# LoRA B rows packed into three operands filled by indirect DMAs, and the h sums moved to GpSimd

## The reference

```python
def lora_linear(x, W, A, B, idx):            # A[idx], B[idx]: one adapter a sequence, rank 16
    return x @ W + (x @ A[idx]) @ B[idx]
gate = lora_linear(x, Wg, Ag, Bg, idx)       # 512 -> 2048
up   = lora_linear(x, Wu, Au, Bu, idx)       # 512 -> 2048
h    = silu(gate) * up
x1   = x + lora_linear(h, Wd, Ad, Bd, idx)   # 2048 -> 512
out  = x1 + per-sequence 64x64 mix of x1 with weights[idx]
```

## Time and profile before

| | us |
|---|---|
| median of 3 runs | 1187.9 (1187.41 to 1190.95) |
| the profiled execution, its own time | 1185.85 |
| its span in the trace | 1184.2 |
| PE busy | 1152.3 (97%) |
| DVE busy | 968.9 (82%) |
| ACT busy | 587.8 (50%) |
| POOL busy | 243.1 (21%) |

### The profile page before, as it was taken

The page is one execution under the profiler, slowest core; times in us unless marked ns, Lnnn a source line. Parts: engine busy times, 40 slices in busy tenths (PEclk is TensorE's granted clock), DMA queues, the critical chain, the costliest instruction groups (busy, mean ns, idle before and its releaser), DMA issues.

```text
span 1184.2 us, 22189 instructions
## 1 busy us (share of the span) xinstructions
PE 1152.3 (97%) x6726; PEld 1026.4 (87%) x6726; DVE 968.9 (82%) x1639; ACT 587.8 (50%) x958; POOL 243.1 (21%) x390
## 2 busy tenths in 40 slices
PE   7899999999999999999999999997999999999998
PEld 5788888888888888888888888887999999999997
DVE  6988898988898988889898999986777667767774
ACT  6555454654454645445465455554444444444442
POOL 3133111123211124311111111112323212321220
PEclk9999999999999999999999999999999999999999
DMA  6485455566555468545558676587777777677771
GB/s 212 140 263 175 139 163 157 177 232 174 161 173 155 134 196 297 178 136 166 155 183 278 177 219 201 160 282 250 266 232 246 244 267 241 233 257 263 250 253 58
DMA packets 147496, 241.05 MB, mean 204 GB/s; under 512 B 21458, under 2 KB 90194, under 8 KB 147250
## 3 DMA queue, kind: packets, MB, share of 16 engines
q1 hardware_dynamic: 124912, 180.94, 48.1%
q0 software_dynamic: 21744, 57.57, 15.3%
q10 hardware_dynamic: 722, 1.13, 0.3%
HBM read 169.30 MB, written 70.25 MB: 202 GB/s over the span
## 4 chain that ended last, share of the span: by engine, by line
PE 82%; DVE 7%; DMA 3%; ACT 3%; issue 3%; SPq 1%; DVEq 0%; ACTq 0%
PE ps L1363 16%; PE ps L1364 16%; PE ps L1365 15%; PE ps L1374 9%; PE ps L1531 7%; PE ps L1533 7%; PE ps L1532 7%; DMA h_raw<-h_dram 3%; PE ps L1392 2%; DVE hl L854 1%; ACT xo_hi L561 1%; ACT hh L561 1%; DVE w_lo L854 1%; DVE xst L865 1%; SPq L194 1%
## 5 line engine op out<-in xcount | busy, mean ns | idle before, releaser
L1363 PE MATMUL ps<-xo_hi,w_hi 128*128 128x512 f32 x882 | 350.0, 397 | 3.8 <-ACT u_s L630 3.1
L1364 PE MATMUL ps<-xo_lo,w_hi 128*128 128x512 f32 x882 | 346.1, 392 | 0.0
L1365 PE MATMUL ps<-xo_hi,w_lo 128*128 128x512 f32 x882 | 343.4, 389 | 0.0
L447 POOL DMA_DIRECT2D h_dram<-hs x128 | 96.2, 756 | 542.3 <-DVE hs L992 274.6
L854 DVE TENSOR_TENSOR hl<-h_raw,hh 128x1024 fp32r<-128x1024 f32 x112 | 136.9, 1223 | 82.8 <-ACT hh L561 81.8
L1365 PEld LDWEIGHTS ps<-xo_hi,w_lo 128*128 128x128 f32 x882 | 165.7, 188 | 36.8
L1363 PEld LDWEIGHTS ps<-xo_hi,w_hi 128*128 128x128 f32 x882 | 166.5, 189 | 33.9 <-ACT u_s L630 5.2
L1364 PEld LDWEIGHTS ps<-xo_lo,w_hi 128*128 128x128 f32 x882 | 166.5, 189 | 25.3
L1374 PEld LDWEIGHTS ps<-t_st,bq 128*128 128x128 f32 x1024 | 156.2, 189 | 22.6 <-issue 2.3
L561 ACT ACTIVATE hh<-h_raw 128x1024 fp32r<-128x1024 f32 x112 | 118.0, 1053 | 114.2 <-DMA h_raw<-h_dram 72.5
L1374 PE MATMUL ps<-t_st,bq 128*128 128x256 f32 x1024 | 162.6, 282 | 1.9 <-DVE t_st L854 1.9
(11 more groups left out here) (160 smaller groups left out, 2333.6 us busy)
## 6 DMA issues: line engine op xcount, KB each, us to landing
h_raw<-h_dram SPq DMA_DIRECT2D x112, 512.0 KB, 5.4
bq_raw<-b_twice SPq DMA_DIRECT2D x512, 64.0 KB, 2.2
h_dram<-hs POOLq DMA_DIRECT2D x128, 256.0 KB, 4.2
raw<-packed SPq DMA_DIRECT2D x58, 512.0 KB, 4.6
h_dram<-h_f SPq DMA_DIRECT2D x96, 256.0 KB, 3.1
ad_raw<-a_d SPq DMA_DIRECT2D x64, 128.0 KB, 2.2
xs<-x POOLq DMA_DIRECT2D x16, 512.0 KB, 4.9
y_out_dram<-xs POOLq DMA_DIRECT2D x30, 256.0 KB, 4.7
```

Of the source, the lines that this page charges most:

```text
L447: pool.dma_start(h_dram[PPG * g:PPG * (g + 1), op, :, k, :].rearrange("q p t -> p q t"), tile[:, col:col + HALF].rearrange("p (q t) -> p q ...
L1363: pe.matmul(bank, st[0], mv[0], start=start and kk == 0, stop=False, skip_group_check=True)
L1364: pe.matmul(bank, st[0], mv[1], start=False, stop=False, skip_group_check=True)
L1365: m = pe.matmul(bank, st[1], mv[0], start=False, stop=kk == 1, skip_group_check=True)
```

## The change

- The B rows of a pair (eight slots, two steps) stand in three operands of 128 rows instead of four, and `lora` issues three matmuls of 256 columns instead of four (`PARTS` = 3). A pair has four units of two slots (32 rows), and each unit needs three blocks of 32 rows: B low by t high, B high by t high, B high by t low. These 12 blocks fill the three operands. Operands 0 and 2 have low parts of B in rows 0 to 63 and high parts in rows 64 to 127, operand 1 has high parts only. The output columns of neighbouring operands overlap by half.
- Each operand is filled by one indirect DMA of 128 rows of 2 KB, issued by POOL (`gather_b`): three a step at the head of POOL's step, in place of the eight gathers a step from SP. The row numbers are made once at the start, by two POOL instructions on a table that ACT's queue loads. POOL's first loads of A rows are halved, the others go to SP.
- `bq_hi` rounds rows 0 to 63 of operands 0 and 2 into a buffer of its own, `bq_lo` (DVE) subtracts, and a new `bq_rest` on ACT, two instructions, rounds the rest. PE waits for `bq_rest_done` too.
- The four h sums are made by POOL instead of DVE, each right before its store.
- `order_a` becomes two copies of half the size, `t_mask`, `t_hi` and `t_lo` become 2, 3 and 2 instructions (before 1, 2 and 2) of other shapes, DVE clears part of `t_st` at the start, and some buffers move.

```diff
-            def gather(n, b):
-                g, k = divmod(n, PIECES)
-                sp.dma_start(bq_raw[n % 2][b % QS:P:QS, b // QS, 1, :, :].rearrange("r k c -> r (k c)"),
-                             b_twice[piece_of(g, k), bass.ds(slot_numbers[g * SLOTS + b], 1)].rearrange("a r c -> (a r) c"))\
-                    .then_inc(bq_in[2 * b // SLOTS][n % 2], 16)
...
-                if s >= 2 and s // 2 + 1 < GROUPS * PIECES:
-                    gather_pair(s // 2 + 1, 1 - s % 2)
...
             def order_a(g, q):
-                pool.wait_ge(a_in[q], 16 * QS * (g + 1))
+                pool.wait_ge(a_in[q], 16 * QS * g)
                 pool.wait_ge(t_done, g * QUADS + q)
-                pool.tensor_copy(aq[0][:, :, :, :], a_raw[0][:, :, :, :].rearrange("p s k r -> p k r s")).then_inc(a_ordered, 1)
+                for i in range(2):
+                    two = 2 * (1 - i if q % 2 == 0 else i)
+                    m = pool.tensor_copy(aq[0][:, :, i, :, :],
+                                         a_raw[g % 2][:, two:two + 2, :, :].rearrange("p s k r -> p k r s"))
+                m.then_inc(a_ordered, 1)
...
             def store_s3(n):
+                pool.wait_ge(h1_done, 2 * n + 1)
+                pool.wait_ge(h2_done, 2 * n + 1)
+                if n:
+                    pool.wait_ge(h_stored[HS3], 16 * n)
+                pool.tensor_tensor(hs3[:, :], h_f[0][:, 0:HALF], h_f[0][:, HALF:GT], ALU.subtract).then_inc(hs3_done, 1)
                 pool.wait_ge(hs3_done, n + 1)
                 store_sum(2 * n, HS3, hs3, 0)
...
+            def gather_b(n, pair):
+                g, k = divmod(n, PIECES)
+                if n >= 2:
+                    pool.wait_ge(p4_done, 2 * n - 2)
+                for part in range(PARTS):
+                    i = (g * 2 + pair) * PARTS + part
+                    pool.indirect_dma_start(bq_raw[n % 2][:, pair, part, :, :].rearrange("r k c -> r (k c)"), None,
+                                            b_table[piece_of(g, k)],
+                                            bass.IndirectOffsetOnAxis(ap=b_rows[:, i:i + 1], axis=0))\
+                        .then_inc(bq_in[pair][n % 2], 16)
...
+            pool.wait_ge(rows_in, 32)
+            pool.tensor_scalar(b_rows[:, :], b_rows[:, :], RANK, None, ALU.mult).then_inc(rows_scaled, 1)
+            pool.wait_ge(rows_scaled, 1)
+            pool.tensor_tensor(b_rows[:, :], b_rows[:, :], rank_of[:, :], ALU.add).then_inc(rows_done, 1)
             pool.wait_ge(idx_in, 16)
-            for q in range(QUADS):
-                gather_a(0, q)
+            gather_a(0, 0)
+            gather_a(0, 1)
+            pool.wait_ge(rows_done, 1)
+            gather_b(0, 0)
+            gather_b(0, 1)
+            gather_b(1, 1)
+            gather_b(1, 0)
             for s in range(1, STEPS):
                 g, c = divmod(s, CH)
+                if s >= 2 and s // 2 + 1 < GROUPS * PIECES:
+                    gather_b(s // 2 + 1, 1 - s % 2)
                 if g + 1 < GROUPS and 4 <= c < 8:
                     order_a(g + 1, c - 4)
...
             def bq_hi(n, pair):
-                q = slice(2 * pair, 2 * pair + 2)
                 act.wait_ge(bq_in[pair][n % 2], GATHER * (n // 2 + 1))
-                if n >= 2:
-                    act.wait_ge(p4_done, 2 * n - 2)
-                hi(bq[n % 2][:, q, 0, :, :], bq_raw[n % 2][:, q, 1, :, :]).then_inc(bq_hi_done, 1)
+                act.wait_ge(bq_lo_done, bq_turn(n, pair))
+                hi(bq_high[0:64, :, :, :], bq_raw[n % 2][0:64, pair, 0:PARTS:2, :, :]).then_inc(bq_hi_done, 1)
+
+            def bq_rest(n, pair):
+                hi(bq[n % 2][:, pair, 1, :, :], bq_raw[n % 2][:, pair, 1, :, :])
+                hi(bq[n % 2][64:P, pair, 0:PARTS:2, :, :], bq_raw[n % 2][64:P, pair, 0:PARTS:2, :, :]).then_inc(bq_rest_done, 1)
...
                 if more:
                     w_hi_sum(s + 1, 1)
+                bq_rest((s + 1) // 2, s % 2)
...
-                if s % 2 == 0:
-                    make_s1(s // 2 - 1)
-                    make_s2(s // 2 - 1)
-                elif not last:
-                    make_s3(s // 2)
-                    if s >= 3:
-                        make_s4(s // 2 - 1)
...
-                for part in range(2):
-                    for i in range(2):
-                        q = pair * 2 + i
-                        m = pe.matmul(bank[:, i * QT:(i + 1) * QT], b[:, q, part, c % PIECE, u * P:(u + 1) * P],
-                                      t_st[u][g % 2][:, q * QT:(q + 1) * QT], start=start and part == i == 0,
-                                      stop=part == i == 1, skip_group_check=True)
+                for i in range(PARTS):
+                    m = pe.matmul(bank[:, i * P:i * P + QT], b[:, pair, i, c % PIECE, u * P:(u + 1) * P],
+                                  t_st[g % 2][:, pair, i, u, :], start=start and i == 0, stop=i == PARTS - 1,
+                                  skip_group_check=True)
...
                 if s % PIECE == 0:
                     pe.wait_ge(bq_lo_done, s + 2)
+                    pe.wait_ge(bq_rest_done, s + 2)
                 lora(RB[par], s, 0, 0, False).then_inc(p2_done, 1)
```

More of the change, by code:

```diff
@@ L27 @@
 PIECES = CH // PIECE
-GATHER = SLOTS // 2 * 16
+PARTS = 3
+GATHER = PARTS * 16
 PAIRS, KC = 16, CH // 2
@@ L746, in _ @@
             bq_hi(0, 0)
+            bq_rest(0, 0)
             order_a_first(2)
@@ L754, in _ @@
             bq_hi(0, 1)
+            bq_rest(0, 1)
             t_hi(0, 3)
@@ L1168, in x_first @@
                 x_lo(0, XOPS.index(op))
+            for i in range(2):
+                for pair in range(2):
+                    m = dve.memset(t_st[i][:, pair, 1, :, :].bitcast(F32), 0.0)
+            m.then_inc(t_zeroed, 1)
             x_first(B11)
@@ L1632 @@
         "idx": ar(np.asarray(itok_B_0_7).reshape(1, BATCH)),
+        "adapter_rows": ar(np.asarray(itok_B_0_7).astype(np.int32, copy=False)[seqs].reshape(P, GROUPS * 2 * PARTS)),
+        "rank_rows": ar(np.broadcast_to((rows % 32 // 2).astype(np.int32)[:, None], (P, GROUPS * 2 * PARTS))),
         "packed": ar(np.concatenate([quarter(L0_cond_Wg, 0), quarter(L0_cond_Wg, 1), quarter(L0_cond_Wu, 1),
```

214 lines of the change are left out of this document (112 added, 102 removed).

## The result

The changed kernel takes 1292.57 us (median of 4 runs, 1290.54 to 1294.12), the kernel before 1188.92 beside it (1187.41 to 1190.95): a ratio of 1.0874, 95% interval 1.0856 to 1.0891. I had forecast 1196.6 with a range of 1167 to 1235. The sign is right; the time lies 96 us above the forecast and 58 above the range.

The account below looks back on a forecast made before the run. PE's matmuls were taken to bound the first phase. Terms -30.2 + 16.3 + 9 + 3 + 5.6 + 5 gave +8.7 us: 1194.6, and with 2.05 from profiled run to median, 1196.6 us; range 1167 to 1235.

Parts of the forecast that it names:

- Elsewhere, +3: Outside the A phases: DVE's idle 0.87 us before `make_h2` mostly absorbs waits on POOL; +3 us (0 to 20).
- the second rival: First phase: each POOL sum holds DVE a whole 0.8 us, so DVE becomes the bound; 1217 us, chance 0.09.
- Matmuls, -30.2: PE's LoRA: 1024 matmuls become 768 at 0.118 us each, a step becomes 11.05 us; -30.2 us.
- Indirect DMAs, 1.15: POOL's gathers of B: 1.15 us each, three a step being 3.45 us (1.65 to 5.9).
- A sum with its store, 2.62: POOL's queue: a sum of 1.21, own wait of 0.65 and store of 0.76 cost 2.62 us.
- The queue in A steps, +16.3: Steps with A loads: POOL's late sums delay DVE, then PE, 5.4 us in each of three groups; +16.3 us.
- the mutual waits there, +9: A phases: DVE and POOL exclude each other, 0.25 us for some 12 POOL instructions a phase; +9 us.
- `bq_rest`, +5.6: ACT's new instructions make PE's LoRA wait 0.2 us in 28 even steps outside A phases; +5.6 us (0 to 9).
- Start, +5: Kernel start: `bq_rest` and longer `t_hi` on ACT, and POOL's row numbers, delay PE's second lora; +5 us (0 to 9).
- Nothing for the rest: SP's fewer issues, more B bytes, gather landings and the phase boundary: priced at nothing, the boundary within 2 us.
- Rival 1: The matmul saving stands because indirect DMAs and POOL's own wait are cheaper; faster, 1169 to 1180 us, chance 0.33.

Follow-up runs that it names:

- experiment 1: The changed kernel with the four h sums back on DVE, everything else as changed: 1194.76 us (ratio 1.0057).
- experiment 4: The changed kernel with each of POOL's sums left out and replaced by one copy of its first operand: 1199.26 us (ratio 1.0089).
- experiment 5: The changed kernel with each of POOL's sums replaced by two one-input copies, the second waiting for the first: 1224.95 us (ratio 1.0306).
- experiment 7: The changed kernel with sums on DVE and the first instruction of `bq_rest` moved ahead of `keep_u2` on ACT: 1188.69 us (ratio 1.0006).
- experiment 9: The changed kernel with sums on DVE, start reordered, `bq_rest` split early in even steps only and behind x operands at boundaries: 1184.84 us (ratio 0.9978).
- 11: The changed kernel with POOL's sums placed beside DVE's PSUM instructions, `bq_rest` split and the start reordered: 1210.92 us (ratio 1.0203).
- kernel 14: The changed kernel with POOL's sums placed beside DVE's PSUM instructions, boundaries included, `bq_rest` split, start reordered, loads of A on SP: 1180.24 us (ratio 0.9933).

## Why the prediction was wrong

**The step that failed** is the one that reads "Elsewhere DVE has the idle 0.87 before `make_h2` and a little more, used up where it adds x or Wd: **+3** (0 to 20)". The mechanism was in the text, and even as the second rival; its price was mis-sized, and with it the place where it decides. In place of 3 us the steps outside of A lost 44.8 us and the boundaries 11.0 (the changed kernel less experiment 1). I took 0.8 us for a sum, from a copy of 128x512 beside one `w_add`. A copy has one input, though. The runs showed that it is the wrong row to read it from: contiguous one-input copies cost the kernel 4.5 us in all (experiment 4), two-input sums 97.8. In steps 12 and 13 above a sum costs DVE 1.1 to 1.8 us. The groups of the changed kernel say the same over the whole of it:

```profile
L912 DVE TENSOR_TENSOR bq<-bq_raw,bq_high 64x1024 fp32r<-64x1024 f32 x64 | 115.1, 1799 | 7.4 <-ACT bq_high L605 7.3
L912 DVE TENSOR_TENSOR w_lo<-wsum,w_hi 128x512 fp32r<-128x512 f32 x114 | 89.1, 815 | 2.0 <-ACT w_hi L605 1.9
L912 DVE TENSOR_TENSOR w_lo<-raw,w_hi 128x768 fp32r<-128x768 f32 x57 | 84.6, 1483 | 0.0
L948 DVE TENSOR_TENSOR wsum<-raw,wsum 128x256 f32<-128x256 f32 x57 | 49.4, 866 | 2.0
L912 DVE TENSOR_TENSOR xo_lo<-xst,xo_hi 128x1024 fp32r<-128x1024 f32 x29 | 46.5, 1627 | 13.0 <-ACT xo_hi L605 12.9
...
L942 DVE TENSOR_TENSOR wsum<-raw 128x256 f32<-128x256 f32 x57 | 40.6, 712 | 0.0
```

With DVE's sums the six are 77.5, 76.7, 54.2, 24.3, 34.7 and 23.9 us busy. The differences add up to 134 us, 1.05 for each of 128 sums, those included that fell on nothing. DVE gave up 0.69 us a sum. So it is not relieved, it has 0.36 us more to do for each; and the hold falls just ahead of what PE waits for, `bq_lo` and `v`. The same six are only 41 us busier with one copy for each sum (experiment 4) and 43 with two (5), 0.3 us a sum or a pair. That two copies hold DVE no longer than one says that it isn't the time that POOL is busy as such; and that 41 us cost the kernel 4.5 and 134 cost it 97.8 says that DVE has room for some of it.

Of the 96 us that the forecast missed, 69.5 lie in the sums (97.8 where the terms 16.3, 9 and 3 make 28.3) and 25 in the rest of the change (+6 in experiment 1, where -30.2, 5.6 and 5 make -19.6).

The Trainium skill (SBUF — State Buffer, Who interferes with whom) says that a DVE instruction with two SBUF inputs contends with a GpSimd instruction that reads SBUF, and that one with at most one SBUF input, outside of the 2-port modes, doesn't. By that rule the placed sums should hold nobody; the trace agrees, 0.69 us. The prediction cited the rule and then averaged it down to half an instruction.

**Point by point.**

- *Matmuls, -30.2.* Right where nothing else is late: there steps are 11.04 to 11.06 in place of 11.52 (experiments 7, 9, 11, 14). In the A steps none of it is left even with DVE's sums (228.2 against 228.3); c = 5, 7, 8 and 9 take it up (13.2, 13.2, 12.3 and 11.6 to 11.9 us where 12.8 and 11.05 are PE's own).
- *Indirect DMAs, 1.15.* Near, but low: 1.30 from start to start in the rows above (413.42, 414.74, 416.04), 0.95 to 1.02 each and 0.30 between. Over the whole trace it is 1.33 in the median and 1.53 on average, since those beside DVE instructions with two SBUF inputs take longer (1.78 at 422.14, 2.88 at most). On average that is 1.1 us a step more than taken.
- *A sum with its store, 2.62.* Near: 1.31 + 0.30 + 0.81 = 2.42. The sum itself is longer than both the 1.21 that I took and the estimate of 1.12; the own wait is 0.30, not 0.65.
- *The queue in A steps, +16.3, and the mutual waits there, +9.* The mechanism is right in each of its links, the size too small. Two copies in place of a sum, which keep POOL longer, cost 22.7 us there (experiment 5), the sums 41.5 (269.7 less 228.2). That the 22.7 are near the 25.3 of the two terms is luck: the rest of the 41.5 is the hold.
- *Elsewhere, +3.* It is 462.1 - 417.3 = 44.8 in the other steps and 11.0 at the boundaries, 55.8 in all.
- *`bq_rest`, +5.6.* The waits are 28, as said, and the profile shows 5.0 us for them; but with a wait of 0.17 the step takes 0.40 more. The LoRA starts 0.56 us behind the matmul ahead of it (400.89), in experiment 7 0.22 (399.17), and the next product 0.43 behind the LoRA in place of 0.39. 28 times 0.40 are 11.2; experiment 7 confirms 0.40 in the 16 such steps of "other".
- *Start, +5.* 11.4 up to the LoRA of step 2 (68.2 less 56.8). The loads of A start 6.9 us later (10.61 against 3.67 in the kernel before), which I had mentioned and not priced; but moving them back brings only 1.2, as the gather of B then comes last.
- *Nothing for the rest.* Wrong at the boundaries: 76.1 against 71.5 even with DVE's sums, 4.6 us. ACT's `bq_rest` stands ahead of the x operands there, but with it behind them (experiment 9) it is still 76.4. That its 1.7 us are what is late either way is likely and not shown, since no run is without it. Wrong in c = 8 too, which takes 12.3 us in place of 11.05 with DVE's sums, 3.8 in the three groups; the cause stays open. Right in that no late gather of B starves PE in the steps.
- *The second rival* (1217) had the right cause. At 1.6 a sum in place of 0.8 its own working gives 10.0 - 1.33 + 3.2 + 0.87 = 12.7 us a step with nothing for x or Wd, and 25.7 us for the two steps from 413.72 to 439.45 were measured, 12.9 each. A chance of 0.09 for it was too little for a rule that I had at hand, and the range (to 1235) covers it at 0.8 only.
- *Rival 1's* 1171 to 1180 is not reached by the change even without the hold: 1194.8, and 1184.8 with ACT's order mended. Only kernel 14, 1180.2, comes there.

Open is why the time that a DVE instruction has run before a sum begins is lost, so that a single sum can hold it for more than its own 1.31 us (1.77 at 417.00); the trace shows the lengths, no run was made for the cause. The rise of the end by 4 us wasn't followed up either.

## What to carry to other kernels

Before work is moved from DVE to POOL, count its SBUF inputs and those of what DVE does at that moment: the price of a two-input sum here was mostly 1.1 to 1.8 us on DVE beside instructions with two SBUF inputs and nothing beside instructions that read PSUM. Place it by a semaphore of DVE, not by when its data is there; a wait more in POOL's queue, with the stores behind it, took 73 us off. And an unknown price is to be bounded by the same number of inputs, not by the same shape.

A saving on the bounding engine shows only in the steps in which nothing else is close behind: of 30.7 us (64 times 0.48) the kernel of experiment 9 kept 3, since start (65.5 us for 56.8), A steps (228.4 for 228.3) and boundaries (76.4 for 71.5) were bounded by others.
